# Small parts of split fp32r products multiplied as f16 copies, with a new instruction order, in a decoder layer

## The chip, the cores and the metric

One core of one Trainium2 chip runs the whole program. The metric is the device time of one execution in microseconds (us); each kernel was run several times and the median is given.

## What is computed

One pre-norm decoder layer in fp32 on x of 64 sequences × 128 tokens × 256. Cut to what matters:

```python
# self-attention: 64 sequences, one head, width 256
raw = (Q @ K.T) * scale                      # Q, K, V from layernorm(x)
w_attn = softmax(where(causal, -inf, raw)) @ V
c_attn = softmax(Q @ mean4(K).T * scale) @ mean4(V)
s_attn = softmax(scatter(top_k(raw, 64))) @ V  # 0 where not among the 64 largest
x = x + ((w_attn + c_attn + s_attn) / 3) @ Wo + bo
# cross-attention: 16 heads of 64, keys and values from ctx
x = x + (softmax(q @ k.T + mask) @ v) @ Wo
# feed-forward, both linear layers quantised per tensor to 8 bits
x = x + qlinear(gelu(qlinear(layernorm(x), w1, b1)), w2, b2)
```

The top-64 choice and the rounding in the quantised layers depend on small differences, so products are made to nearly full fp32 precision.

## The kernel before

**Tiling.** The 64 sequences go in 32 pairs. A pair's tiles are 128 partitions wide; an output bank of PSUM holds 128 × 512 fp32. `attentions` (L391) holds everything but the feed-forward stage, which `feed_forward` (L1600) does afterwards for all pairs.

**Pipeline.** Each engine has a function `body(i, front, back, ahead)` (L516 SP, L574 POOL, L728 PE, L1055 ACT, L1257 DVE), called for i = −1, 0, then in a loop of 30 (`Fori(1, PAIRS - 1)`), then 31 and 32. In one body three pairs are in work: *front* is pair i (cross-attention's keys, values, queries and scores, self-attention's output), *back* is pair i−1 (weighted values, heads, output product, x2 and its normalising), *ahead* is pair i+1 (layernorm of x, folded self-attention up to the mixed probabilities). The order in each body is written out by hand; engines meet only through semaphores. The bodies before the loop do part of the work in `EARLY_JOBS` while weights are still being prepared (`prepare_weights`, L116).

**Split products.** Each operand is kept as an fp32r upper part HI and an fp32r remainder LO. A product is three matmuls, HI·HI, HI·LO and LO·HI:

```python
def split_products(pe, out, lhs, rhs, last=True, first=True):
    pe.matmul(out, lhs[HI], rhs[HI], start=first, stop=False)      # L111
    pe.matmul(out, lhs[HI], rhs[LO], start=False, stop=False)      # L112
    return pe.matmul(out, lhs[LO], rhs[HI], start=False, stop=last)  # L113
```

The products that use it: `keys` and `queries` (four jobs each, 256 columns), `values` (four jobs, 512 columns), `output` (two, 256 columns), `fold_query` (the folded query g), `fold_value` (two), `raw_scores` (256 columns for each sequence: its own 128 keys and the other sequence's), and, on f16 operands, `weigh` (66 columns, "pv" in the order of the back) and `scores`. ACT writes HI from PSUM (`hi`, L1076; heads L1096), DVE writes LO from PSUM minus HI and frees the bank (`lo`, L1274; heads L1308). For keys and values ACT writes HI and an fp32 copy, and POOL makes LO (L581).

**DVE's other steps in a body.** `statistics` (L1231) and `normalise` (L1241) of a layernorm; `add_mask` (L1286, four heads a step, with their maxima); `row_sums` and `divide` (L1295, L1301, four heads); eight `top_round`s (L1335, L1338); `window_and_compressed` (L1347 to L1353); `mix` (L1367 to L1380) of the three softmaxes; `second_residual` (L1400, which makes x2) and `x2_statistics` (L1406, L1410). POOL subtracts the maxima (`shift`, L589), makes the LO part of the exponentials (`exp_lo`, L595) and the deviations of the layernorms (`x2_deviation`, L606 to L612, and L559 to L561).

**SP's queue.** In a body SP issues, each behind its own semaphore waits and in this order:

```python
if ahead: load_x(i + 1)                       # L497
if front: load_mask(1, i); load_mask(0, i)
if ahead: load_context(i + 1)
if back:  store_x2(0, i - 1); store_x2(1, i - 1)   # L510
if back:  store_normed(i - 1)                 # L514, waits for ACT's normalise_x2 (L1106)
```

So the load of the next x_in stands behind the store of the normalised x2. `statistics` of x_in waits for that load, and `load_x` for `normalise` of the x_in before.

## Time and profile before

| | |
|---|---|
| median of 3 runs | 1675.04 us (1672.29 to 1675.15) |
| profiled execution | 1671.48 us |
| its span, first to last instruction | 1669.4 us |
| mean granted TensorE clock | 0.983 of 2.4 GHz |
| PE busy | 1573.6 us, 94% |
| DVE busy | 1461.2 us, 88% |
| ACT / POOL busy | 1060.9 / 1051.2 us, 64% / 63% |
| DMA engines | 43 GB/s on average |

A line of the trace gives start, duration, engine, source line, operation, output<-inputs, shapes and type. Matmuls are pipelined, so their time is read from the distance between starts and not from the duration of one; where several stand in one line ("x15"), the time of the line is that of all of them. A bracket at a line's end is how long the engine stood idle before it, and what released it. The stretch from 131.9 to 1343.1 us is 28 turns of the loop. In trace lines the names of buffers have lost their numbers: `x2` reads x, `normed2` reads normed, `xn1` reads xn.

### The profile page before, as it was taken

Reading aid. Unit: us, or ns where it says so; the run is one execution under the profiler, and the core shown is the slowest. Engines: PE = TensorE matmul, PEld = TensorE weight load, DVE = VectorE, ACT = ScalarE, POOL = GpSimd, SP = SyncE. Lnnn points to the kernel's source line nnn. Section 1 sums busy time; section 2 is a strip of 40 time slices with the busy share of each in tenths; the row PEclk is TensorE's granted clock in tenths of the full one; section 3 lists DMA queues with packets and bytes.
Section 4 is the critical chain, followed back from the end, with each engine's and each line's share of the span. In section 5 each row is a group of like instructions: output and inputs, shape, how many; then the busy total and the mean of one; then the engine's idle time right before and its main releaser. Section 6 shows DMA issues by size and latency. Waiting matters only on the chain.

```text
span 1669.4 us, 51921 instructions
## 1 busy us (share of the span) xinstructions
PE 1573.6 (94%) x16058; PEld 1401.0 (84%) x16058; DVE 1461.2 (88%) x6184; ACT 1060.9 (64%) x2205; POOL 1051.2 (63%) x1168
## 2 busy tenths in 40 slices
PE   6799999999999999999999999999999999778898
PEld 5689999999999999999999999999999998644465
DVE  4889999999999999999999999999999996679876
ACT  4456666666666666666666666666666666469875
POOL 4557777777777777777777777777777776621000
PEclk9999999999999999999999999999999999789999
DMA  6000000000000000000000000000000000221155
GB/s 211 8 15 29 28 28 28 25 28 28 28 27 22 26 28 28 28 28 28 28 28 28 28 28 22 22 28 28 25 28 28 28 28 17 90 85 51 60 178 166
DMA packets 77732, 71.01 MB, mean 43 GB/s; under 512 B 6272, under 2 KB 77184, under 8 KB 77696
## 3 DMA queue, kind: packets, MB, share of 16 engines
q1 hardware_dynamic: 76736, 70.41, 13.4%
q8 instruction: 21, 0.34, 0.1%
q10 hardware_dynamic: 960, 0.13, 0.1%
q14 instruction: 15, 0.12, 0.0%
HBM read 45.36 MB, written 25.17 MB: 42 GB/s over the span
## 4 chain that ended last, share of the span: by engine, by line
PE 73%; DVE 14%; ACT 6%; issue 4%; POOL 1%; DMA 0%; ACTq 0%; DVEq 0%; SPq 0%; POOLq 0%
PE banks L111 21%; PE banks L112 18%; PE banks L113 18%; PE banks L868 5%; DVE tile_max L2010 4%; PE banks L848 3%; PE banks L892 3%; DVE xn L1241 3%; PE banks L1901 2%; ACT normed L1106 2%; DVE x L1390 1%; DVE ctx_t L1274 1%; ACT ctx_t L1076 1%; DVE kept L2022 1%; PE banks L747 1%
## 5 line engine op out<-in xcount | busy, mean ns | idle before, releaser
L589 POOL TENSOR_TENSOR shifted<-scores,score_max 128x512 f32<-128x512 f32 x256 | 266.9, 1043 | 200.6 <-DVE score_max L1286 159.9
L595 POOL TENSOR_TENSOR exp_t<-exp_copy,exp_t 128x512 f16<-128x512 f32 x256 | 302.5, 1182 | 60.6 <-ACT exp_copy L1091 60.6
L1286 DVE CUSTOM_DVE_ANT_0 scores<-banks,mask 128x128 f32<-128x128 f32 x1024 | 235.0, 286 | 11.6 <-issue 6.0
L1076 ACT ACTIVATE q_t<-banks 128x512 f16<-128x512 f32 x128 | 76.5, 598 | 224.0 <-PE banks L113 224.0
L581 POOL TENSOR_TENSOR v_nat<-kv_copy,v_nat 128x512 f16<-128x512 f32 x124 | 138.8, 1130 | 105.2 <-ACT kv_copy L1079 105.2
L111 PE MATMUL banks<-ctx_t,cross_Wk 128*128 128x256 f32 x512 | 154.7, 302 | 21.8 <-DVE ctx_t L1274 18.5
L1089 ACT ACTIVATE exp_t<-banks 128x512 f16<-128x512 f32 x256 | 155.9, 609 | 6.2 <-PE banks L113 3.8
L1091 ACT ACTIVATE exp_copy<-banks 128x512 f32<-128x512 f32 x256 | 158.6, 620 | 0.0
L868 PE MATMUL banks<-ident,shifted 128*128 128x128 f32 x1024 | 153.8, 279 | 3.9 <-POOL shifted L589 2.8
L111 PE MATMUL banks<-xn_t,cross_Wq 128*128 128x256 f32 x512 | 153.1, 299 | 2.7 <-POOL cross_Wo L269 1.6
L1079 ACT ACTIVATE kv_copy<-banks 128x512 f32<-128x512 f32 x248 | 150.9, 608 | 0.0
L1096 ACT ACTIVATE heads_t<-banks 128x512 fp32r<-128x512 f32 x128 | 76.5, 598 | 115.2 <-PE banks L892 115.2
L111 PE MATMUL banks<-cross_Wo,heads_t 128*128 128x256 f32 x512 | 147.8, 289 | 1.6 <-DVE heads_t L1308 1.6
L112 PE MATMUL banks<-ctx_t,cross_Wk 128*128 128x256 f32 x512 | 145.2, 284 | 0.0
L581 POOL TENSOR_TENSOR k_t<-kv_copy,k_t 128x512 f16<-128x512 f32 x124 | 145.1, 1170 | 0.0
L113 PE MATMUL banks<-xn_t,cross_Wq 128*128 128x256 f32 x512 | 145.1, 283 | 0.0
L113 PE MATMUL banks<-ctx_t,cross_Wk 128*128 128x256 f32 x512 | 145.0, 283 | 0.0
L112 PE MATMUL banks<-xn_t,cross_Wq 128*128 128x256 f32 x512 | 144.9, 283 | 0.0
L112 PE MATMUL banks<-cross_Wo,heads_t 128*128 128x256 f32 x512 | 144.3, 282 | 0.0
L113 PE MATMUL banks<-cross_Wo,heads_t 128*128 128x256 f32 x512 | 144.2, 282 | 0.0
L111 PE MATMUL banks<-v_nat,exp_t 128*128 128x66 f16 x1024 | 123.0, 196 | 6.5 <-POOL exp_t L595 3.3
L111 PEld LDWEIGHTS banks<-ctx_t,cross_Wk 128*128 128x128 f32 x512 | 97.8, 191 | 35.2 <-DVE ctx_t L1274 24.6
(261 smaller groups left out, 5661.8 us busy)
## 6 DMA issues: line engine op xcount, KB each, us to landing
x_in<-in_x_dram SPq DMA_DIRECT2D x32, 256.0 KB, 2.8
ctx_in<-in_ctx_dram SPq DMA_DIRECT2D x32, 256.0 KB, 2.7
x_residual<-x SPq DMA_DIRECT2D x64, 128.0 KB, 1.7
x_normalised<-normed SPq DMA_DIRECT2D x32, 256.0 KB, 2.1
shared<-x_normalised SPq DMA_DIRECT2D x8, 1024.0 KB, 5.3
shared<-x_residual SPq DMA_DIRECT2D x16, 512.0 KB, 3.8
out_dram<-shared SPq DMA_DIRECT2D x16, 512.0 KB, 2.9
mask<-in_fside_Bx1xSxS_dram SPq DMA_DIRECT2D x64, 64.0 KB, 1.8
```

The lines of the kernel that those rows point to most:

```text
L111: pe.matmul(out, lhs[HI], rhs[HI], start=first, stop=False)
L112: pe.matmul(out, lhs[HI], rhs[LO], start=False, stop=False)
L113: return pe.matmul(out, lhs[LO], rhs[HI], start=False, stop=last)
L581: pool.tensor_tensor(hilo(dst, *at)[LO], src, hilo(dst, *at)[HI], ALU.subtract).then_inc(kv_split, 1)
L589: pool.tensor_tensor(shifted[:, q % 2], scores[:, q % 2], score_max[:, q % 2, :].unsqueeze(2).to_broadcast([P, QUAD, P]), ALU.subtract).th ...
L595: pool.tensor_tensor(exp_t[:, q % 2, LO], exp_copy[:, q % 2], exp_t[:, q % 2, HI], ALU.subtract).then_inc(exp_split, 1)
L868: mm = pe.transpose(et_bank(q)[:, tile(h)], shifted[:, q % 2, h, :], ident)
L1076: op = act.activation(hilo(dst, *at)[HI], src, ACT.Copy)
L1079: act.activation(kv_copy[:, KV.index(k) % 2, :], fj_bank(k), ACT.Copy).then_inc(fj_free[k % 2], steps(k, same_bank(k), front, back, ahead, ...
L1089: act.activation(exp_t[:, q % 2, HI], et_bank(q).rearrange("p (h s) -> p h s", h=QUAD), ACT.Exp)
L1091: act.activation(exp_copy[:, q % 2], et_bank(q).rearrange("p (h s) -> p h s", h=QUAD), ACT.Exp).then_inc(et_free, 1)
L1286: op = dve.tensor_tensor_reduce(scores[:, q % 2, h, :], sc_bank(q)[:, tile(h)], mask[:, b, :], 1.0, NEG, ALU.add, ALU.max, score_max[:, q ...
```

## The change

1. **Small products in f16.** `half_products` first issues all HI·HI products of a job in fp32r, then for each term two products on f16 tiles: the f16 copy of HI on one side with the f16 LO of the other. LO tiles of keys', queries', values', outputs', folded and raw-score products are now f16. LO parts of weights are scaled up by 64 (256 for the folded ones), the copies of activations down by as much. `attend` and `weigh` keep the three-product form.
2. **Raw scores.** The small products cover only the sequence's own 128 keys.
3. **Copies.** ACT makes nine more SBUF-to-SBUF copies 128 × 512 in each body: of the transposed x (two), g, x1's transposed, the context, and four of the heads. In the preparation ACT makes 18 copies of weights and DVE scales 16 tiles of 512 columns.
4. **Order.** The job tuple, the back's order and the hand-written order on all five engines are new. The early jobs are only x, the four keys, g and the raw scores; the first pair's values are now made in body 0.

Cut to its core (`half` and `copy_heads` are new on ACT, `cross_halves` and `cross_up` in the preparation):

```diff
-(J_PT1, J_K0, J_K1, J_PT0, J_AO, J_X, J_K2, J_V0, J_V1, J_G, J_K3, J_X1, J_RAW, J_Q1,
- J_Q0, J_Q2, J_Q3, J_VV0, J_VV1, J_VV2, J_VV3, J_CTX) = range(22)
+(J_PT0, J_K0, J_K1, J_PT1, J_K2, J_AO, J_X, J_K3, J_V1, J_G, J_V0, J_RAW, J_X1, J_VV0,
+ J_Q1, J_Q0, J_Q3, J_VV1, J_Q2, J_VV2, J_VV3, J_CTX) = range(22)
...
-EARLY_JOBS = (J_X, J_G) + KV + (J_RAW,)
+EARLY_JOBS = (J_X, *J_K, J_G, J_RAW)
...
+def half_products(pe, terms):
+
+
+
+    for n, (out, left, right, *_) in enumerate(terms):
+        pe.matmul(out, left[0], right[0], start=(n == 0), stop=False, skip_group_check=True)
+    for n, (out, left, right, *narrow) in enumerate(terms):
+        small, cut = narrow[0] if narrow else (out, lambda t: t)
+        pe.matmul(small, left[1], cut(right[2]), start=False, stop=False, skip_group_check=True)
+        mm = pe.matmul(small, left[2], cut(right[1]), start=False, stop=(n == len(terms) - 1), skip_group_check=True)
+    return mm
...
+    def cross_halves(act, k0, k1):
+        act.wait_ge(cross_copied, k1)
+        for k in range(k0, k1):
+            act.activation(cross_at(k)[1], cross_at(k)[0].bitcast(F32), ACT.Copy).then_inc(cross_half, 1)
...
+            pool.tensor_tensor(cross_copy[:, k % COPIES, :], cross_copy[:, k % COPIES, :], cross_at(k)[0].bitcast(F32),
+                               ALU.subtract).then_inc(cross_low, 1)
+
+    def cross_up(dve, k0, k1):
+        for k in range(k0, k1):
+            dve.wait_ge(cross_low, k + 1)
+            dve.tensor_scalar(cross_at(k)[2], cross_copy[:, k % COPIES, :], UP, None, ALU.mult).then_inc(cross_split, 1)
...
             if front:
+                load_mask(0, i)
                 load_mask(1, i)
-                load_mask(0, i)
             if ahead:
                 load_context(i + 1)
             if back:
+                store_x2(1, i - 1)
                 store_x2(0, i - 1)
-                store_x2(1, i - 1)
                 store_normed(i - 1)
...
+        def raw_products(bank):
+
+            own = lambda b: (bank[:, b * 2 * P + b * P:b * 2 * P + (b + 1) * P], lambda t: t[:, tok(b)])
+            return half_products(pe, [(bank[:, b * 2 * P:(b + 1) * 2 * P], three(g_t, kt, tok(b)),
+                                       three(xn_t, kt, copy=PLAIN), own(b)) for b in range(2) for kt in range(DT)])
...
                 bank = begin(k)
-                for m, mt in enumerate(out_tiles):
-                    for kt in range(DT):
-                        mm = split_products(pe, bank[:, m * 2 * P:(m + 1) * 2 * P], hilo(w, kt, tile(mt)),
-                                            hilo(src, kt), first=(kt == 0), last=(kt == DT - 1))
-                done(mm, k)
+                done(half_products(pe, [(bank[:, m * 2 * P:(m + 1) * 2 * P], three(w, kt, tile(mt)), three(src, kt))
...
+        def half(k, part=HALF):
+
+            (top, halves), ready, scale = {J_X: (xn_t, plain_x if part == PLAIN else half_x, 1.0 / FOLD_UP),
+                                           J_G: (g_t, half_g, 1.0), J_CTX: (ctx_t, half_ctx, 1.0 / UP),
+                                           J_X1: (xn1_t, half_x1, 1.0 / UP)}[k]
+            act.activation(halves[:, part], top[:].bitcast(F32), ACT.Copy,
+                           scale=1.0 if part == PLAIN else scale).then_inc(ready, 1)
...
+            def copy_heads(c, n):
+                at = slice(4 * (c % 2), 4 * (c % 2) + 4)
+                act.wait_ge(bj_hi, bj_his(n, c))
+                act.activation(heads_t[1][:, HALF, at, :], heads_t[0][:, at, :].bitcast(F32), ACT.Copy,
+                               scale=1.0 / UP).then_inc(half_heads, 1)
...
+            if front:
+                exponential(1, i)
                 hi(J_VV3, i)
+            if ahead:
+                hi(J_CTX, i + 1)
+                copy(J_CTX, i + 1)
             if back and not front:
                 ffn_of["prime"](act)
             if back:
                 normalise_x2(i - 1)
-            if ahead:
-                hi(J_CTX, i + 1)
...
                     add_mask(2, i)
+                    add_mask(3, i)
                 if back:
                     second_residual(1, i - 1)
                     x2_statistics(i - 1)
-                if front:
-                    add_mask(3, i)
                 if ahead:
                     mix(i + 1)
+                if ahead and not front:
+                    early_lo(J_G)
                 if ahead and front:
                     lo(J_CTX, i + 1)
+                if front:
+                    add_mask(4, i)
                 if back:
                     largest_of_x2(i - 1)
-                if front:
-                    add_mask(4, i)
```

The order of instructions at three places in the loop, on DVE. `ISA` rows with `scores` and `score_max` are one head of `add_mask`.

DVE, the end of the loop body, before: the last head of `add_mask(3)`, then `mix`, the LO part of the context, and the largest of x2. The second residual and the x2 statistics stand ahead of this `add_mask(3)`.

```order
L1286 ISA score_max 128x1
L1367 RECIPROCAL inv_sums<-sums 128x6
L1369 TENSOR_TENSOR weights<-inv_sums,third 128x6
L1372 TENSOR_SCALAR win_in<-win_in,weights 128x128 x2
L1375 REGISTER_ALU
L1376 SCALAR_TENSOR_TENSOR sparse_in<-sparse_in,weights,win_in 128x128 x2
L1380 SCALAR_TENSOR_TENSOR probs<-comp_e,weights,sparse_in 128x128 x2
L1259 REGISTER_ALU
L1274 TENSOR_TENSOR ctx_t<-banks,ctx_t 128x512
L1415 ISA
L1415 TENSOR_REDUCE x2_far<-normed2 128x2
```

DVE, the same place after the change: `second_residual(1)` and `x2_statistics` now follow `add_mask(3)`; `mix` follows them.

```order
L1379 ISA score_max 128x1
L1488 REGISTER_ALU
L1493 TENSOR_TENSOR x2<-banks,x1_old 128x256
L107 REGISTER_ALU
L1499 BN_STATS stats2<-x2 128x6 x2
L1503 BN_AGGR moments2<-stats2 128x2 x2
L1460 RECIPROCAL inv_sums<-sums 128x6
L1462 TENSOR_TENSOR weights<-inv_sums,third 128x6
L1465 TENSOR_SCALAR win_in<-win_in,weights 128x128 x2
L1468 REGISTER_ALU
L1469 SCALAR_TENSOR_TENSOR sparse_in<-sparse_in,weights,win_in 128x128 x2
L1473 SCALAR_TENSOR_TENSOR probs<-comp_e,weights,sparse_in 128x128 x2
```

One step of four masks has moved ahead of the x2 statistics; the mix has stayed behind them.

DVE, the head of the loop body, before: the last head of `add_mask(5)`, then the statistics of x_in, then `row_sums(0)` (`inv_den`).

```order
L1286 ISA score_max 128x1
L1227 ISA
L1231 BN_STATS stats<-x_in 128x6 x2
L1235 BN_AGGR moments<-stats 128x2 x2
L1294 ISA
L1295 RECIPROCAL inv_den<-banks 128x4
```

DVE, the same place after the change: `row_sums(0)` and `divide(0)` (`heads_out`) come first.

```order
L1379 ISA score_max 128x1
L1387 ISA
L1388 RECIPROCAL inv_den<-banks 128x4
L1392 REGISTER_ALU
L1394 TENSOR_TENSOR heads_out<-banks,inv_den 128x4x64
L1320 ISA
L1324 BN_STATS stats<-x_in 128x6 x2
L1328 BN_AGGR moments<-stats 128x2 x2
```

The statistics of x_in, which wait for its load, have moved behind one row sum and one division.

DVE, `window_and_compressed`, before: behind the top round 6 and the LO part of queries 3 (`q_t`).

```order
L1338 MATCH_REPLACE left<-top8,left 128x128
L104 REGISTER_ALU
L1338 MATCH_REPLACE left<-top8,left 128x128
L1259 REGISTER_ALU
L1274 TENSOR_TENSOR q_t<-banks,q_t 128x512
L1347 ISA win_in,maxes<-raw,causal 128x128
L1347 ISA maxes 128x1
L1347 ISA win_in,maxes<-raw,causal 128x128
L1347 ISA maxes 128x1
L1350 TENSOR_REDUCE comp_in<-raw 128x64
L1353 TENSOR_REDUCE maxes<-comp_in 128x2
```

DVE, the same step after the change: behind the LO part of x1 (`xn1_t_half`) and top round 1.

```order
L1367 TENSOR_TENSOR xn1_t_half<-banks,xn1_t 128x512
L1428 MAX top8<-left 128x8 x2
L107 REGISTER_ALU
L1431 MATCH_REPLACE left<-top8,left 128x128
L107 REGISTER_ALU
L1431 MATCH_REPLACE left<-top8,left 128x128
L1440 ISA win_in,maxes<-raw,causal 128x128
L1440 ISA maxes 128x1
L1440 ISA win_in,maxes<-raw,causal 128x128
L1440 ISA maxes 128x1
L1443 TENSOR_REDUCE comp_in<-raw 128x64
L1446 TENSOR_REDUCE maxes<-comp_in 128x2
```

The window and the compressed scores now come five top rounds earlier.

## Rows read from the trace of the kernel before

**Rows 1.** The page: busy time of the engines; the chain that ended last.

```profile
PE 1573.6 (94%) x16058; PEld 1401.0 (84%) x16058; DVE 1461.2 (88%) x6184; ACT 1060.9 (64%) x2205; POOL 1051.2 (63%) x1168
...
PE 73%; DVE 14%; ACT 6%; issue 4%; POOL 1%; DMA 0%; ACTq 0%; DVEq 0%; SPq 0%; POOLq 0%
```

**Rows 2.** Windows: span, PE, PEld, DVE, ACT, POOL busy, PEclk, DMA share, GB/s; 28 pairs, one pair.

```profile
131.90:1343.10 1211.20, 1191.37 (x12998) 1104.02 (x12993) 1117.76 (x5210) 771.64 (x1765) 882.04 (x981) 1.00 0.09 27
703.31:746.53 43.22, 42.51 (x468) 39.45 (x467) 39.87 (x187) 27.56 (x63) 31.51 (x36) 1.00 0.09 27
```

**Rows 3.** Timeline of PE: start, us, engine, line, operation (an output job, pv, queries).

```profile
719.93 0.28 PE L113 MATMUL banks<-cross_Wo,heads_t 128*128 128x256 f32 x1
...
721.01 0.28 PE L113 MATMUL banks<-cross_Wo,heads_t 128*128 128x256 f32 x1
...
721.47 0.19 PE L113 MATMUL banks<-v_nat,exp_t 128*128 128x66 f16 x1
721.50 0.36 PE L111 MATMUL banks<-xn_t,cross_Wq 128*128 128x256 f32 x1
721.70 0.28 PE L112 MATMUL banks<-xn_t,cross_Wq 128*128 128x256 f32 x1
```

**Rows 4.** Timeline of PE: values, 512 columns.

```profile
729.66 0.39 PE L112 MATMUL banks<-cross_Wv,ctx_t 128*128 128x512 f32 x1
...
730.58 0.40 PE L113 MATMUL banks<-cross_Wv,ctx_t 128*128 128x512 f32 x1
```

**Rows 5.** Timeline of PE: bf16 products of the feed-forward stage.

```profile
1581.50 1.03 PE L1875 MATMUL banks<-xq_t,w_q 128*128 128x512 bf16 x4
1582.36 1.80 PE L1901 MATMUL banks<-w_q,shared 128*128 128x256 bf16 x15
```

**Rows 6.** Waits of DVE, then PE, 100 to 1390: total us, times, longest us.

```profile
DVE x L1400 <- PE banks L113: 11.6, 30, 0.4
DVE stats L1231 <- DMA x_in<-in_x_dram: 7.9, 28, 0.4
DVE row_rq L1272 <- ACT v_fold L1076: 6.5, 29, 0.2
DVE scores L1286 <- issue: 6.0, 31, 0.2
DVE inv_den L1295 <- PE banks L113: 5.8, 23, 0.4
...
PE banks L111 <- DVE ctx_t L1274: 18.5, 30, 0.6
```

**Rows 7.** Timeline of DVE, ACT and SP at the end of a pair.

```profile
735.28 0.25 DVE L1410 BATCH_NORM_AGGREGATE moments<-stats 128x2 f32<-128x6 f32 x2
...
736.40 0.19 DVE L1367 RECIPROCAL inv_sums<-sums 128x6 f32<-128x6 f32 x1
...
737.61 1.09 ACT L1106 ACTIVATE normed<-x,shift,rstd 128x256 f32<-128x256 f32 x2
...
738.84 0.38 SPq L514 DMA_DIRECT2D x_normalised<-normed  x1
739.88 0.41 SPq L497 DMA_DIRECT2D x_in<-in_x_dram  x1
...
742.62 0.75 DVE L1231 BATCH_NORM_STATS2 stats<-x_in 128x6 f32<-128x256 f32 x2 [0.23 <-DMA x_in<-in_x_dram]
```

**Rows 8.** Timeline of DVE: one of the `divide` steps.

```profile
700.53 0.42 DVE L1301 TENSOR_TENSOR heads_out<-banks,inv_den 128x256 f32<-128x256 f32 x1
```

**Rows 9.** Groups of ACT, 1430 to 1669: busy us, mean ns of one; idle before.

```profile
L1954 ACT ACTIVATE shared<-kept 128x1024 bf16<-128x1024 f32 x22 | 22.1, 1050 | 1.5 <-DVE kept L2022 1.5
```

**Rows 10.** Single lines of DVE: ns min/median/max, first and last start.

```profile
L1241 DVE TENSOR_SCALAR xn<-x_in,moments,rstd x64: 405/698/1366, 13.5 to 1351.9; 128x256 f32<-128x256 f32 x64
...
L1347 DVE CUSTOM_DVE_ANT_0 win_in<-raw,causal x64: 279/284/506, 45.7 to 1377.3; 128x128 f32<-128x128 f32 x64
...
L1380 DVE SCALAR_TENSOR_TENSOR probs<-comp_e,weights,sparse_in x64: 342/347/1218, 54.7 to 1387.0; 128x128 f32<-128x128 f32 x64
```

More of the change, by code:

```diff
@@ L984, in body @@
             if front:
-                queries(3, i)
-            if front and not early:
-                values(0, i)
-            if front:
-                exp_transpose(0, i)
+                values(1, i)
             if back:
@@ L992, in body @@
             if front:
+                queries(2, i)
+                exp_transpose(0, i)
+                values(2, i)
                 scores(1, i)
-            if front and not early:
-                values(1, i)
             if back:
@@ L1040, in early_job @@
                 op.then_inc(early_hi, 1)
+                act.wait_ge(early_hi, 1)
+                half(k)
                 return
@@ L1489, in body @@
                     ffn_of["weight_peak"](dve, 1)
+                if back:
+                    add_mask(7, i - 1)
+                    row_sums(3, i - 1)
+                    divide(3, i - 1)
                 if ahead:
```

469 lines of the change are left out of this document (259 added, 210 removed).

## Prediction

> **What bounds the kernel now.** I read the page first [rows 1]. TensorE (PE) is busy for 94% of the span and VectorE (DVE) for 88%; the chain that ended last lies on PE for 73% and on DVE for 14%. That looks like a PE kernel with DVE close behind, so a cheaper PE is worth what DVE lets through. The windows give the pace: 1211.20 us hold 28 pairs, 43.26 each, and the single pair from 703.31 takes 43.22, with PE busy 42.51, DVE 39.87, ACT 27.56 and POOL 31.51, and the clock at 1.00, which is 2.4 GHz [rows 2]. ACT has 15.7 us free in each pair. Busy shares do not say what DVE would allow, so I looked at the waits [rows 6]: in 30 pairs DVE waits for PE (x, inv_den), for ACT (row_rq), and once a pair for the DMA of x_in; the longest of those is 0.4 us, so every party is nearly just in time.
>
> The last of these waits matters, because it belongs to a **ring** [rows 7]. The x2 statistics end at 735.28 + 0.25 = 735.53. POOL then makes the deviation, ACT normalises (737.61 to 738.70), SP stores the result at 738.84, and only behind that store, in SP's order, stands the load of the next x_in, at 739.88. It lands when DVE's BATCH_NORM_STATS2 starts, at 742.62. So the stretch from x2 statistics to landed x_in is 7.09 us. The rest of the pair, 43.22 − 7.09 = 36.13 us, is what DVE does in its own order from those statistics of x_in to the next x2 statistics. The pace cannot be shorter than these two together, whatever PE does.
>
> **PE's part.** Steps between starts: fp32r, 256 columns, (721.01 − 719.93)/9 = 0.120 us [rows 3]; fp32r, 512 columns, (730.58 − 729.66)/4 = 0.230 [rows 4]. The trace has no f16 product of that width; the nearest are bf16, and I take theirs: (1.80 − 0.28)/14 = 0.109 for 256 columns and (1.03 − 0.40)/3 = 0.21 for 512 [rows 5], the single durations 0.28 and 0.40 being those of [rows 3, 4]. Per pair 112 small products of 256 columns (keys 32, queries 32, outputs 32, fold_query 8, fold_value 8) save 0.011 each, 1.23 us. The 16 of the values save 0.02 each, 0.32. The 8 of the raw scores shrink to 128 columns; a 66-column product steps 0.03 (721.47 to 721.50) [rows 3], so on the line from 66 to 256 columns 128 cost 0.056, and 8 × (0.120 − 0.056) = 0.51. Against it: the first fp32r product behind 66-column f16 ones takes 0.20 to its next (721.50 to 721.70), 0.08 more than usual [rows 3]. The new order puts five jobs there (keys 0, the second fold_value, fold_query, raw scores, queries 1) where two stood: 3 × 0.08 = 0.24. Sum: −1.8 us, a PE pace of **41.4**. The bounds: if the 0.08 belongs to any change from f16 to fp32r, up to 16 more of the 18 jobs pay it, 1.3 instead of 0.24, and the gain is 0.75; no row gives more than 2.1 (without the 0.24). I take the low price since the nearest row is a 66-column one, whose stationary loads have nothing to hide behind.
>
> The trace's 0.21 us at 512 columns is the number used. The Trainium skill (TensorE: Matmul & The Clock Gate, Back-to-back issue gap) states about 81 ns for 128 columns and 131 ns for 512 in a stream of load and product pairs. By it the values would save 16 × (230 − 131) ns = 1.6 us and the raw scores 8 × (120 − 81) ns = 0.3, 1.1 us a pair more in all on PE; rows 5 disagree, and the measurement decides.
>
> **DVE's part.** The order rows show what changes inside the 36.13 us section. Out of it goes row_sums and divide 0, now ahead of the x_in statistics: 0.42 [rows 8] and a reciprocal, 0.6. Into it comes add_mask(3), now ahead of second_residual(1): the same step of four heads runs from 735.53 to 736.40, 0.87 [rows 7]. The waits in it for PE, ACT and issue, 11.6 + 6.5 + 6.0 + 5.8 = 29.9 us in 30 pairs, 1.0 a pair [rows 6], mostly vanish when PE runs ahead: at most 1.0, at least 0.2 (the longest single kind staying); I take 0.9. Section: 36.13 − 0.6 + 0.87 − 0.9 = 35.5. Ring: ACT now does context HI and its copy before the normalising; a 1024-wide SBUF-to-SBUF copy takes 1.05 [rows 9], so a 512-wide one about 0.6 (an estimate, a 512-wide half and some fixed part), but it stands where ACT is idle anyway while POOL makes the deviation, so I book 0.1. Ring: 7.2. Together 42.7; with the masks' order on SP, mask 0 before 1 and store 1 before 0, at nothing (DMA share 0.09 [rows 2]), I take a pace of **42.6**, 0.6 under the present one. That is below the cover PE gives away (41.4), so DVE, waiting for x_in, ends the pair.
>
> The nine ACT copies cost 9 × 0.6 = 5.4 us of the 15.7 free: nothing, unless one stands ahead of something late. If that cover were gone, a copy's 0.6 would go on the pair. PE's 0.6 us wait for the LO part of ctx_t [rows 6] becomes longer, not shorter, since PE arrives earlier; it is no longer on the path.
>
> **Outside the loop.** ACT gets 18 weight copies, DVE 16 scalings of 512; values jobs leave the early stretch and their loads of POOL with them. Bounds: all 16 scalings on the path beside POOL, 16 × 0.9, +14; all the left-out early jobs saved, −6. I take +3. The feed-forward stage is untouched.
>
> **Sum.** 30 × (−0.6) + 3 = −15. The profiled execution took 1671.5 (span 1669.4); the median of three runs is 1675.0, 0.2% above, and I put the change on the median: **1660**. Within this case the low end has every wait gone, no 0.1 for the copy and −6 outside, 30 × (−0.7) − 6 = −27; the high end keeps all but 0.2 of the waits, a pace of 43.3 that rounds to no gain, and +3: **1648 to 1678**.
>
> **Rivals.** *A, the forecast above: 0.46.*
>
> *B, PE's pace is reached (0.22).* The section is full of DVE operations that POOL slows: normalising x_in takes 0.405 us at least, 0.70 at the median and 1.37 at most [rows 10]. If the new order lets two such pairs run clear, DVE gets back the 1.2 us between 42.6 and 41.4. Then 30 × (−1.8) + 3 = −51: **1624**. For it: window_and_compressed, lo and masks are all shuffled against POOL. Against it: POOL is busy 31.5 of 43 us, so most places collide.
>
> *C, slower (0.20): DVE meets POOL.* window_and_compressed moves from behind queries 3, late in the pair, to right behind the second top-k round, where POOL has exponentials' LO, keys 3 and values 0. One window operation takes 0.284 at the median and 0.506 at most [rows 10], a factor 1.8, which over the 1.0 us of the step is +0.8. Probs goes from 0.347 to 1.218 [rows 10], four such operations in the mix; the x_in pair from 0.8 to the 1.66 it already sometimes takes would be +0.7 more. Section and ring become 42.7 + 1.5 = 44.2: 30 × 1.0 + 3 = +33, **1708**. It decides against the change from 0.6 us of added blocking a pair upward. The trace shows such blocking at 1.218 against 0.347 us.
>
> The Trainium skill (SBUF — State Buffer, SBUF: two separate sides) has the rule behind it: a DVE operation with two SBUF inputs or in a 2-port mode and a GpSimd operation exclude each other for a whole instruction. The trace agrees with it for probs (two SBUF inputs). For the window operation it shows 0.506.
>
> *D, no gain appears (0.12).* The normalising moves by a whole copy's 0.6 rather than 0.1: 35.5 + 7.7 = 43.2, and the time is 1675 + 3 = **1678**. Or the changes between fp32r and f16 cost 0.08 in both directions: 18 jobs × 2 × 0.08 = 2.9 against 2.1 saved, a PE pace of 44.0 and 30 × 0.8 + 3 = +27, 1702. For it: every small product now sits between fp32r groups, and no row shows such a change inside a job. Against it: the change from f16 to fp32r behind a 66-column product is the only one that reads longer in [rows 3].
>
> **Chances.** About 0.2% (3.3 us) is what a measurement can tell from no change. Faster: A nearly whole (0.40) and B (0.22), 0.62. Same: the thin end of A and half of D, 0.09. Slower: C, half of D, and the end of A in which start-up and one late copy eat the gain, 0.29. The range runs from B's 1624 to 1702, leaving out the faster half of B and the far part of C. A's own is 1648 to 1678.
>
> **What would show it.** In the changed profile the pair should last about 42.6 us at clock 1.00, PE busy about 40.7, and the wait of DVE for x_in should grow from 0.26 us a pair to 1 or more, while DVE's waits for PE (x, inv_den) shrink: then A. If that wait is absent and PE is busy all but 0.7 us of the pair, B. If DVE's busy time per pair rises above 40.5 with window or probs operations near 0.5 or 1.2 us, C. Steps of the f16 products should read 0.109 and 0.21; a step of 0.12 or more there, or 0.20 at the first of every fp32r group, makes the PE term wrong and speaks for D. The forecast is wrong if the pair is over 43.2, or under 42.

## The result and the profile after

| | before | changed |
|---|---|---|
| median | 1674.3 us (1672.3 to 1675.2, 6 runs) | 1667.3 us (1665.6 to 1668.0, 6 runs) |
| ratio, 95% interval | | 0.9958 (0.9945 to 0.9971) |
| profiled execution: time, span | 1671.5, 1669.4 us | 1667.8, 1666.0 us |
| pace in the loop, from the context transposes of pair to pair | 43.25 us | 42.68 us |

The change makes the kernel 7.0 us faster, 0.42%, where 15 were forecast. The page after, busy time of the engines and the chain that ended last (compare [rows 1]):

```profile
PE 1554.7 (93%) x16058; PEld 1245.2 (75%) x16058; DVE 1468.4 (88%) x6202; ACT 1223.2 (73%) x2511; POOL 1062.8 (64%) x1168
...
PE 39%; DVE 34%; issue 12%; ACT 7%; DMA 4%; POOL 2%; DVEq 1%; SPq 1%; ACTq 0%; POOLq 0%
```

PE has lost 19 us of busy time in all, ACT has gained 162 (most of it the nine copies a pair), and the chain no longer lies on PE for 73% but on PE for 39 and DVE for 34. The windows after, of 28 pairs and of one (compare [rows 2]; span, then PE, PEld, DVE, ACT and POOL busy, clock):

```profile
141.80:1336.90 1195.10, 1169.46 (x12993) 964.56 (x12992) 1117.69 (x5209) 905.06 (x2017) 893.01 (x981) 1.00 0.09 28
696.60:739.30 42.70, 41.77 (x465) 34.44 (x464) 39.92 (x187) 32.34 (x73) 31.92 (x36) 1.00 0.08 28
```

The 28 pairs last 42.68 us each against 43.26, the single one 42.70 against 43.22. In the single one PE's busy time fell only from 42.51 to 41.77, and DVE's did not change (39.87 and 39.92). The waits of DVE from 100 to 1390 us (compare [rows 6]; total, times, longest), with the longest one before, which [rows 6] leave out, ahead of those after:

```profile
DVE ctx_t L1274 <- ACT ctx_t L1076: 26.0, 30, 0.9
```

```profile
DVE stats L1324 <- DMA x_in<-in_x_dram: 41.0, 29, 1.5
DVE raw L1412 <- PE banks L128: 6.4, 30, 0.2
DVE inv_den L1388 <- PE banks L116: 4.5, 2, 2.9
```

and those of PE:

```profile
PE banks L124 <- DVE g_t_half L1355: 10.1, 30, 0.3
PE banks L950 <- DVE heads_out L1394: 3.4, 15, 0.3
```

DVE's wait for x_in grew from 7.9 us in 28 pairs to 41.0 in 29; its waits for x and row_rq have all but gone (x 0.6 us in all, once). This is the picture that the forecast had described, but most of the growth has another source. Before, DVE also stood 0.87 us a pair for ACT's HI part of the context, between the x2 statistics and the statistics of x_in. ACT now makes that part ahead of the normalising, and this wait has gone (0.5 us, once). So DVE's idle time in that stretch rose from 0.87 + 0.26 = 1.13 to 1.41 us a pair, by 0.3 and not by 1.15. The ring, on the timelines of DVE, ACT, SP and DVE again (compare [rows 7]):

```profile
739.88 0.25 DVE L1503 BATCH_NORM_AGGREGATE moments<-stats 128x2 f32<-128x6 f32 x2
...
742.28 1.10 ACT L1183 ACTIVATE normed<-x,shift,rstd 128x256 f32<-128x256 f32 x2
...
743.51 0.38 SPq L571 DMA_DIRECT2D x_normalised<-normed  x1
744.55 0.41 SPq L554 DMA_DIRECT2D x_in<-in_x_dram  x1
...
747.28 0.75 DVE L1324 BATCH_NORM_STATS2 stats<-x_in 128x6 f32<-128x256 f32 x2 [1.35 <-DMA x_in<-in_x_dram]
```

From the end of the x2 statistics, 739.88 + 0.25 = 740.13, to the landed x_in at 747.28 are 7.15 us, and the rest of the pair, DVE's section, is 42.68 − 7.15 = 35.53. Forecast were 7.2 and 35.5.

What the small products cost PE, and what the entry into a job costs (timeline of PE; compare [rows 3, 5]):

```profile
716.03 0.19 PE L116 MATMUL banks<-v_nat,exp_t 128*128 128x66 f16 x1
716.56 0.71 PE L124 MATMUL banks<-xn_t,g_t 128*128 128x256 f32 x4 [0.34 <-DVE g_t_half L1355]
717.11 0.23 PE L127 MATMUL banks<-xn_t_half,g_t_half 128*128 128x128 f16 x1
...
717.24 0.22 PE L127 MATMUL banks<-xn_t_half,g_t_half 128*128 128x128 f16 x1
...
717.52 0.22 PE L128 MATMUL banks<-xn_t_half,g_t_half 128*128 128x128 f16 x1
...
723.01 0.27 PE L128 MATMUL banks<-xn_t_half,cross_Wq_half 128*128 128x256 f16 x1
723.04 1.19 PE L124 MATMUL banks<-cross_Wo,heads_t 128*128 128x256 f32 x8
724.07 0.28 PE L127 MATMUL banks<-cross_Wo_half,heads_t_half 128*128 128x256 f16 x1
```

In the raw scores the steps are (717.52 − 717.24)/5 = 0.056 us. From the last f16 product of 256 columns at 723.01 over eight fp32r ones to 724.07 are 1.06 us, which is 0.109 + 8 × 0.119: the change from f16 to fp32r costs nothing there. Behind the 66-column product at 716.03 it is otherwise: 0.03 for that product and 0.34 of waiting would put the first raw product at 716.40, it starts at 716.56, and its four take 0.55 instead of 0.48. This entry costs 0.23.

The single lines of DVE (ns min/median/max; compare [rows 10]):

```profile
L1334 DVE TENSOR_SCALAR xn<-x_in,moments,rstd x64: 401/405/411, 13.8 to 1348.6; 128x256 f32<-128x256 f32 x64
L1334 DVE TENSOR_SCALAR xn<-x,moments,rstd x64: 650/1246/1362, 67.5 to 1397.0; 128x256 f32<-128x256 f32 x64
...
L1440 DVE CUSTOM_DVE_ANT_0 win_in<-raw,causal x64: 280/284/1112, 46.0 to 1361.5; 128x128 f32<-128x128 f32 x64
...
L1473 DVE SCALAR_TENSOR_TENSOR probs<-comp_e,weights,sparse_in x64: 337/346/347, 57.8 to 1381.9; 128x128 f32<-128x128 f32 x64
```

Normalising x_in now runs clear of POOL everywhere, 0.405 at the median against 0.698; inside the loop the two operations of a pair went from 1.78 us to 0.81. Normalising x1 does not, 1.246. The window operation stays at 0.284 in nearly all its places although it moved, and probs at 0.346. Another operation took the place of x_in's, the one that forms the sparse scores, before and after:

```profile
L1357 DVE SCALAR_TENSOR_TENSOR sparse_in<-left,raw x32: 425/426/1123, 47.8 to 1380.3; 128x256 f32<-128x256 f32 x32
...
L1450 DVE SCALAR_TENSOR_TENSOR sparse_in<-left,raw x32: 424/1344/1346, 52.6 to 1374.8; 128x256 f32<-128x256 f32 x32
```

It costs 0.92 us more in each pair. In the pair shown above it starts at 734.55, 0.11 us behind an operation of POOL (`exp_lo`). The 0.97 gained at one place and the 0.92 lost at the other are why DVE's busy time did not change.

The start of the program, marked by the transposes of the context of the first, second and third pair (the third stands at the end of the loop's first turn), before:

```profile
34.97 1.05 PE L747 MATMUL banks<-ident,ctx_in 128*128 128x128 f32 x4
...
81.01 1.00 PE L747 MATMUL banks<-ident,ctx_in 128*128 128x128 f32 x4
...
131.95 0.65 PE L747 MATMUL banks<-ident,ctx_in 128*128 128x128 f32 x4
```

and after:

```profile
38.34 0.63 PE L798 MATMUL banks<-ident,ctx_in 128*128 128x128 f32 x4 [0.87 <-DVE raw L1412]
...
90.69 0.60 PE L798 MATMUL banks<-ident,ctx_in 128*128 128x128 f32 x4
...
141.85 0.60 PE L798 MATMUL banks<-ident,ctx_in 128*128 128x128 f32 x4
```

From the first of these marks to the third, called "to the loop" below, the program takes 103.5 us instead of 97.0. Nearly all of the 6.5 lies between the first two, 52.35 us against 46.04: PE is busy there for 37.35 us against 34.76 and idle for 3.7 us more, and the granted clock is 0.80 on average against 0.94. From the second to the third it is 51.16 against 50.94. The waits of PE in the first 142 us, after:

```profile
PE banks L926 <- ACT exp_copy L1168: 5.8, 2, 5.5
PE banks L124 <- DVE g_t_half L1342: 4.9, 1, 4.9
PE banks L124 <- ACT cross_Wk_half L296: 3.3, 1, 3.3
```

and the window from 57 to 81 us before, then after, with the granted clock as its third number from the end:

```profile
57.00:81.00 24.00, 15.84 (x162) 14.22 (x162) 19.52 (x99) 8.96 (x18) 11.96 (x13) 0.93 0.04 12
```

```profile
57.00:81.00 24.00, 16.03 (x92) 13.03 (x93) 16.57 (x61) 17.74 (x37) 12.16 (x11) 0.72 0.00 1
```

PE stood for g's LO part (4.9 us), for weight copies on ACT (3.3) and for an exponential that ACT makes only behind the next pair's softmaxes (5.5). The last of these lies behind the second mark, where PE stood for 4.1 us before the change too (for probs of DVE). In the window from 57 to 81 us the granted clock averaged 0.72 of 2.4 GHz against 0.93: part of it was spent at 1.2 GHz. The clock went to that level at 43.70, inside the 3.3 us of waiting, and again at 57.35, inside the 4.9 us, for 20.5 us in all between the first two marks (5.2 before). The end of the program, from the last such transposes on, takes 286.4 us against 283.1; over all profiles but e7's it takes 283.4 to 287.2 with the changed kernel and its variants, and 283.1 to 285.5 with the one before, so how much of these 3.3 us belongs to the change stays open; the means are 1.3 apart.

### The profile page after: what moved, and what is told of

It reads as the page before. It is cut to its first block, busy times and chain, and to the rows that moved or that the text cites. A ratio compares the mean times of both kernels' runs of the same rounds, so it can differ in the third digit from the quotient of the medians.

```text
span 1666.0 us, 52582 instructions
## 1 busy us (share of the span) xinstructions
PE 1554.7 (93%) x16058; PEld 1245.2 (75%) x16058; DVE 1468.4 (88%) x6202; ACT 1223.2 (73%) x2511; POOL 1062.8 (64%) x1168
## 4 chain that ended last, share of the span: by engine, by line
PE 39%; DVE 34%; issue 12%; ACT 7%; DMA 4%; POOL 2%; DVEq 1%; SPq 1%; ACTq 0%; POOLq 0%
PE banks L124 10%; PE banks L127 8%; PE banks L128 7%; DVE scores L1379 6%; DMA x_in<-in_x_dram 3%; DVE tile_max L2110 3%; DVE sparse_in L1450 2%; DVE heads_t_half L1401 2%; DVE xn L1334 2%; PE banks L926 2%; PE banks L906 2%; DVE left L1431 2%; PE banks L798 2%; PE banks L2001 2%; DVE g_t_half L1355 2%
## 5 line engine op out<-in xcount | busy, mean ns | idle before, releaser
L638 POOL TENSOR_TENSOR v_nat<-kv_copy,v_nat 128x512 f16<-128x512 f32 x128 | 149.3, 1166 | 44.5 <-ACT kv_copy L1146 44.5
L1166 ACT ACTIVATE exp_t<-banks 128x512 f16<-128x512 f32 x256 | 152.4, 595 | 5.7 <-PE banks L116 2.9
L114 PE MATMUL banks<-v_nat,exp_t 128*128 128x66 f16 x1024 | 121.9, 195 | 7.6 <-POOL exp_t L652 3.2
L926 PEld LDWEIGHTS banks<-ident,shifted 128*128 128x128 f32 x1024 | 115.2, 142 | 16.9 <-issue 7.6
L127 PE MATMUL banks<-ctx_t_half,cross_Wk_half 128*128 128x256 f16 x512 | 122.6, 279 | 0.0
L128 PE MATMUL banks<-ctx_t_half,cross_Wk_half 128*128 128x256 f16 x512 | 121.1, 276 | 0.0
L115 PE MATMUL banks<-v_nat,exp_t 128*128 128x66 f16 x1024 | 121.1, 195 | 0.0
L1431 DVE MATCH_REPLACE8 left<-top,left 128x128 f32<-128x128 f32 x448 | 120.2, 276 | 0.0
L114 PEld LDWEIGHTS banks<-v_nat,exp_t 128*128 128x128 f16 x1024 | 94.5, 97 | 34.2 <-issue 17.2
L127 PE MATMUL banks<-xn_t_half,cross_Wq_half 128*128 128x256 f16 x512 | 120.1, 275 | 0.0
L116 PE MATMUL banks<-v_nat,exp_t 128*128 128x66 f16 x1024 | 119.8, 193 | 0.0
L128 PE MATMUL banks<-xn_t_half,cross_Wq_half 128*128 128x256 f16 x512 | 118.7, 273 | 0.0
L127 PE MATMUL banks<-cross_Wo_half,heads_t_half 128*128 128x256 f16 x512 | 118.6, 278 | 0.0
L1143 ACT ACTIVATE k_t<-banks 128x512 f16<-128x512 f32 x124 | 74.0, 597 | 59.7 <-PE banks L128 59.7
```

The source lines that it names most:

```text
L127: pe.matmul(small, left[1], cut(right[2]), start=False, stop=False, skip_group_check=True)
L128: mm = pe.matmul(small, left[2], cut(right[1]), start=False, stop=(n == len(terms) - 1), skip_group_check=True)
L638: pool.tensor_tensor(hilo(dst, *at)[LO], src, hilo(dst, *at)[HI], ALU.subtract).then_inc(kv_split, 1)
L926: mm = pe.transpose(et_bank(q)[:, tile(h)], shifted[:, q % 2, h, :], ident)
L1166: act.activation(exp_t[:, q % 2, HI], et_bank(q).rearrange("p (h s) -> p h s", h=QUAD), ACT.Exp)
L1431: dve.match_replace(left[:, b, :], top8[:, b, :], (raw if r == 0 else left)[:, b, :], NEG).then_inc(top_out, 1)
```

## The experiments

The pace is always the distance of the context transposes from pair to pair in the loop. The changed kernel has 42.68 us and about 1667, the kernel before 43.25 and, run beside each group of experiments, 1672 to 1674. The ratios are to that kernel before. The theories are named in the expectations as they were held then; R and P were the first two.

**The ring cut, first try, in the changed kernel and in the one before.**

```diff
 # SP, end of body
-                store_normed(i - 1)
 # ACT, end of normalise_x2
+                act.wait_ge(normed_ready, n + 2)
+                act.dma_start(normed_pairs[n], normed2[:]).then_inc(normed_free, 16)
```

> The changed kernel with one edit: ACT issues the store of the normalised x2 on its own queue right after making it, so SP's load of the next x_in no longer stands behind it. Theory R (the ring: x2 statistics to landed x_in, 7.15 us, and DVE's section, 35.5, set the pace of 42.68 us): the load starts about 3 us earlier, DVE's wait for x_in falls from 1.42 us a pair to under 0.2, and the pace falls to what PE or DVE allow, 41.4 to 42.1; time 1667 - 30 x (0.6 to 1.3) = 1628 to 1649. Theory P (PE's work sets 42.68 and the wait for x_in is slack): pace stays 42.5 or more and time within 4 us of 1667.

> The same edit in the kernel before. Both theories take that kernel to be at PE's pace (43.2 with PE busy 42.5), with 0.26 us of waiting for x_in a pair. Theory R: the pace moves by 0.3 at most, time 1665 to 1674. If the ring was the bound there already, the pace drops by 0.5 or more, under 1660. Against 1674.3.

Measured: 1679.7 us (ratio 1.0043, 1.0027 to 1.0060), pace 43.25; and in the kernel before 1689.9 (1.0102, 1.0085 to 1.0119), pace 43.75. The waits of DVE, then PE, in the first:

```profile
DVE probs_t L1369 <- ACT probs_t L1143: 20.2, 54, 0.5
...
PE banks L124 <- DVE probs_t L1369: 19.3, 27, 0.7
```

The wait for x_in is gone, but ACT now stands about 1 us at its own store ahead of the probs_t of the next body, DVE behind ACT, and PE behind DVE with 0.7 us a pair. The edit bought one wait with another, so it decides nothing about the ring. It does show that ACT's first operation of a body is on the path.

**The ring cut on SP alone, in both kernels.**

```diff
 # SP, body
-            if ahead:
+            if early:
                 load_x(i + 1)
...
+            if ahead and not last:
+                load_x(i + 2)
+            if back:
                 store_normed(i - 1)
```

Here `early` is body 0 and `last` the loop's last turn, now written out behind it, which has no further x_in to load.

> The changed kernel with one edit on SP alone: the load of the x_in for the pair after next is issued at the end of a body, ahead of the store of the normalised x2 and not behind it. ACT's queue is as in the changed kernel, so what spoiled the run with the store on ACT (1 us more before its first copy of probs_t) is not there. Theory R (a loop of 42.68 us that runs x2 statistics, normalising, store, load, 7.15 us, and then DVE with 12 to 15 us of PE work in its middle): the 1.4 us wait for x_in goes and the pace falls by that or to PE's busy time, 41.6 to 42.2; time 1637 to 1653. Theory P (PE's work and its small waits set the pace): pace 42.5 to 42.7, time 1663 to 1670. Theory K (any change of phase brings new collisions of DVE with POOL): DVE busy above 40.3 us a pair and pace over 42.9.

> The same edit in the kernel before. Theories R and P: that kernel is at PE's pace, its 0.26 us wait for x_in goes and the pace falls by 0.3 at most: 1664 to 1675. Theory K: a pace above 43.4.

Measured: 1665.6 us (0.9952, 0.9936 to 0.9969), pace 42.68 as before the edit; the kernel before 1672.7 (0.9993, 0.9983 to 1.0002), pace 43.22. The waits of DVE in the changed kernel with this edit, 28 pairs:

```profile
DVE x L1487 <- PE banks L116: 17.6, 28, 0.6
DVE inv_den L1392 <- PE banks L116: 12.0, 28, 0.4
DVE probs_t L1371 <- ACT probs_t L1147: 7.4, 28, 0.3
```

The 1.4 us for x_in have become 0.63 for PE's attend (x), 0.43 for PE's pv (inv_den) and 0.26 for ACT's probs_t. Theory R, that the ring alone sets the pace, falls. DVE's timeline shows why, first in the changed kernel, then with the load ahead:

```profile
701.44 0.28 DVE L1367 TENSOR_TENSOR probs_t<-banks,probs_t 128x128 fp32r<-128x128 f32 x1
...
704.70 0.75 DVE L1324 BATCH_NORM_STATS2 stats<-x_in 128x6 f32<-128x256 f32 x2 [1.45 <-DMA x_in<-in_x_dram]
...
707.40 0.69 DVE L1483 TENSOR_TENSOR x<-banks,x_bias 128x512 f32<-128x512 f32 x1
```

```profile
698.44 0.28 DVE L1371 TENSOR_TENSOR probs_t<-banks,probs_t 128x128 fp32r<-128x128 f32 x1
...
704.39 0.69 DVE L1487 TENSOR_TENSOR x<-banks,x_bias 128x512 f32<-128x512 f32 x1 [0.63 <-PE banks L116]
```

From the LO part of probs 0 to the first residual, `x<-banks,x_bias`, are 5.96 us in the one and 5.95 in the other. In the first DVE comes there late from x_in and finds attend just done (its last product ends at 707.36), in the second it comes early and waits for attend. Both paths have the same length within what the trace resolves.

**More and less work on PE.**

```diff
 # e3, raw_products
-                                       three(xn_t, kt, copy=PLAIN), own(b)) for b in range(2) for kt in range(DT)])
+                                       three(xn_t, kt, copy=PLAIN)) for b in range(2) for kt in range(DT)])
 # e11, half_products, for the queries alone
-        pe.matmul(small, left[1], cut(right[2]), start=False, stop=False, skip_group_check=True)
+        if not fewer:
+            pe.matmul(small, left[1], cut(right[2]), start=False, stop=False, skip_group_check=True)
```

> The changed kernel with the small products of the raw scores over all 256 columns again: 8 products a pair go from 0.056 to 0.109 us, 0.42 us more PE work a pair. Theory R: PE has 0.9 us free a pair, pace within 0.1 of 42.68, time 1665 to 1671. Theory P: pace 43.1, time 1680.

> The changed kernel, leaving out one of the two small products of every term of the queries: 16 products of 256 columns a pair, 1.74 us of PE. Theory P2: PE's work sets the pace and with 1.74 less the next bound shows. If the ring of x_in and DVE's section is next, its slack in the changed kernel is the 1.4 us of waiting, and the pace stops near 41.3 with DVE waiting for x_in near 1.3 still; time 1667 - 30 x 1.4 = 1625. If PE still sets it: pace 40.95, time 1615. Theory S: pace 42.6 or more, 1664 to 1668.

Measured: e3 1677.6 us (1.0028, 1.0017 to 1.0039), pace 43.10, that is the whole 0.42. e11 1648.9 (0.9856, 0.9840 to 0.9872), pace 42.21: of 1.74 us taken off PE 0.47 arrive. The waits of DVE in e3, and the window from 151 to 1350 us and DVE's wait in e11:

```profile
DVE stats L1324 <- DMA x_in<-in_x_dram: 37.2, 27, 1.5
DVE raw L1412 <- PE banks L128: 17.9, 28, 0.6
```

```profile
151.00:1350.00 1199.00, 1152.98 (x12724) 933.80 (x12724) 1123.66 (x5279) 919.50 (x2046) 905.03 (x994) 1.00 0.09 28
...
DVE stats L1325 <- DMA x_in<-in_x_dram: 38.3, 28, 1.5
```

In e3 DVE waits 0.6 us for the raw scores instead of 0.2. In e11 PE is busy 1153.0 of 1199 us and idle for the rest, 1.6 us a pair, with DVE's wait for x_in unchanged. Compared step by step, 0.42 of the 0.47 comes where DVE takes a row sum and two LO parts of the queries: it starts them sooner, although the profile lists no wait there, and its busy time falls from 39.92 to 39.53 a pair. So the pace is not PE's work as such. Work on PE counts where DVE waits for its result, and the raw scores are such a place, while most of the queries are not.

**DVE work put outside and inside the stretch in question.**

```diff
+                for c in range(2):
+                    dve.tensor_reduce(at["spare"][:, bass.ds(n * 2 + c, 1)], keep["bo_row"][:], AX, ALU.max)
 # e18: behind lo(J_PT0, i); e19: behind add_mask(3, i), ahead of second_residual(1)
```

> The changed kernel with 0.7 us more of DVE work a pair (two maxima over 256 columns that nothing reads), put behind the LO part of probs 0, where DVE has 1.4 us of waiting for x_in ahead. Theory L: nothing moves, pace 42.68 to 42.75, time 1666 to 1670. If DVE's total work sets the pace: +0.7, time 1689.

> The same 0.7 us of extra DVE work, put behind add_mask(3) and ahead of the second residual, inside the stretch of DVE that theory L has in its loop. Theory L: the whole 0.7 goes on the pace, 43.4, time 1667 + 31 x 0.7 = 1689. If PE's work sets the pace: pace within 0.1 of 42.68, time 1667 to 1670.

Measured: e18 1673.7 us (1.0005, 0.9992 to 1.0018), pace 43.00; e19 1684.1 (1.0075, 1.0048 to 1.0102), pace 43.32. DVE's busy time rose by 0.47 and 0.65 a pair. The waits of e19, DVE then PE, and of e18:

```profile
DVE stats L1325 <- DMA x_in<-in_x_dram: 37.8, 27, 1.5
...
PE banks L872 <- DVE probs L1474: 20.9, 27, 0.8
```

```profile
DVE stats L1325 <- DMA x_in<-in_x_dram: 23.4, 27, 1.0
...
PE banks L799 <- DVE xn L1335: 23.0, 28, 0.8
```

Inside the stretch the whole 0.65 comes out at the pace, PE waits 0.8 us for probs, and the wait for x_in stays at 1.4. Outside it DVE's wait for x_in takes up 0.5, but 0.32 still comes out. This run is not as clean as it was meant to be: one of the two operations that normalise x_in now runs beside POOL and takes 1.25 us instead of 0.41 (at the same time those of x1 run clear, 1.1 less), so PE waits 0.8 us a pair for it, and DVE in turn 0.3 for g (`g_t_half <- ACT g_t`). So e19 comes out as a loop through this stretch wants it; e18 does not tell what the idle time ahead of x_in is worth by itself.

**Steps moved.**

```diff
 # e7, DVE: add_mask(3) behind x2_statistics again
 # e15, DVE: end of body
-                if front:
-                    add_mask(4, i)
 # e15, DVE: head of body, behind lo(J_PT0, i); POOL: shift(4, i - 1) behind exp_lo(1, i - 1)
+                    add_mask(4, i - 1)
 # e10, PE: raw_scores(i + 1) behind exp_transpose(7, i - 1), no more ahead of it
```

> The changed kernel with add_mask(3) back behind second_residual(1) and the x2 statistics on DVE, as before the change. Theory R: DVE's section is 0.87 us shorter, pace 41.8 if nothing else binds, 42.1 if DVE must wait for PE's output product; time 1641 to 1651. Theory P: pace 42.5 or more, time within 4 us of 1667, or slower since the shift behind this mask comes later.

> The changed kernel with add_mask(4) moved on DVE from the end of a body to the next body's head, behind the LO part of probs 0, and POOL's shift 4 moved along behind exp_lo 1. Theory L (a loop of 42.68 us: DVE without a wait from g's LO part and the raw scores to the LO part of probs 0, then PE from keys 0 to attend, then DVE's first residual, normalise and g; the wait for x_in lies beside PE's part and costs nothing): 0.87 us leave DVE's part and fall into DVE's 1.4 us of idle time beside PE's part, so the pace falls by up to 0.87, to 41.9 to 42.2 where PE's work binds; time 1641 to 1654. Theory R is dead; theory G (the pace is no loop but the sum of accidental collisions): any sign, pace 42.3 to 43.5.

> The changed kernel with one pair of neighbours exchanged on PE: raw_scores now stands behind the transposes of scores 7 and not behind pv5. By the starts in the changed kernel's trace an fp32r job behind 66-column products costs PE 0.08 to 0.25 us more than its products, and this one 0.24, while behind transposes of 128 columns it costs nothing; the pv5 to transpose change may take 0.03 to 0.16 back. Theory P2 (PE's work with these entries sets the pace): pace 42.68 falls by 0.1 to 0.24, time 1660 to 1664. Theory S (something that does not depend on PE's entries sets it): pace within 0.03 of 42.68; or raw scores come 0.44 us later and DVE waits: pace up by as much.

All three missed. e7: 1703.0 us (1.0185, 1.0167 to 1.0203), pace 43.83, DVE busy 40.79 a pair instead of 39.92. e15: 1757.1 (1.0512, 1.0484 to 1.0540), pace 44.55 in the first pairs and near 46 later. e10: 1682.6 (1.0059, 1.0042 to 1.0076), pace 43.27, DVE busy 40.49. In e15 this is PE's longest wait:

```profile
PE banks L798 <- DVE xn L1334: 54.1, 27, 2.0
```

POOL's and DVE's steps ahead of the normalising of x_in came later, and PE stood 2.0 us a pair at its transposes. In e10 the 0.23 of the raw entry went, entries of other jobs rose by more, and the raw scores came 0.1 later. What costs the time is one operation of DVE that now meets POOL: the second `win_in<-raw,causal` starts at 725.91, 0.02 us behind POOL's `v_nat`, and takes 1.25 us instead of 0.28, 0.96 a pair, against a pace that rose by 0.59. In e7 it is the first `win_in<-win_in,weights` of the mix, 0.95 instead of 0.29.

The larger part of e7's loss is the ring. POOL's order still has the shift of mask 3 ahead of the deviation of x2. With the mask behind the x2 statistics, POOL waits 1.55 us for its maxima and takes 1.05 for the shift, so the deviation begins 2.13 us behind the end of the statistics (753.84 against 751.71) and not 0.16 (740.29 against 740.13). Averaged over 20 pairs, the stretch from x2 statistics to x_in grows from 7.21 to 9.09 us, the rest of the pair shrinks from 35.47 to 34.73, and their sum is the measured 43.83: the edit did shorten DVE's section, and lengthened the ring by more. Moving one step of this order without the rest costs more than the step is worth.

**Interleaved as before.**

```diff
     for n, (out, left, right, *narrow) in enumerate(terms):
+        pe.matmul(out, left[0], right[0], start=(n == 0), stop=False, skip_group_check=True)
         small, cut = narrow[0] if narrow else (out, lambda t: t)
```

> The changed kernel with each term's two f16 products directly behind its fp32r product, as split_products has them, and not in a group of their own: 64 more changes from f16 to fp32r a pair. If such a change costs PE something everywhere (0.03 to 0.09 us), pace +2 to +5 us and time 1727 to 1820. If it costs only behind 66-column products, time within 4 us of 1667.

Measured: 1682.6 us (1.0058, 1.0041 to 1.0075), pace 43.28, between the two expectations. PE's busy time is 42.60 a pair, 0.83 more, over the 50 extra changes of a pair (68 terms in 18 jobs; the expectation's 64 was too many) 0.02 us each. That all fp32r products stand first is therefore needed: without it the changed kernel would be slower than the one before.

**The start-up.**

```diff
 # e5, DVE, body -1: cross_up(4, 8) from behind raw_scores to the end
 # e6, ACT: self_softmax(0) behind the early job of g; DVE: early_lo(J_G) ahead of mix
 # e13: both
```

> The changed kernel with the second four scalings of cross weights on DVE moved from behind raw_scores of body -1 to the end of that body. In the trace of the changed kernel DVE stands from 38.4 to 42.7 us at them, before the top rounds of pair 0. If these four are what made the start-up longer, 3 to 4.5 us of the 10 come back: 1663 to 1664.5; the loop's pace stays 42.68. If the start-up is set by what PE and ACT do, it stays within 1.5 us of 1667.

> The changed kernel with pair 1's early job for g moved ahead: ACT takes it before the softmaxes of pair 0 and DVE makes its LO part before the mix. PE waited 4.9 us for that LO part at 59 us. If that wait and the 5.5 us of PE at 91 us hang on the lateness of pair 1's raw scores, 4 to 8 us come back: 1659 to 1663; if the lost time lies elsewhere, within 1.5 us of 1667; pace 42.68 either way.

> Both start-up edits together: the second four scalings at the end of body -1, and the early job for g ahead of the softmaxes and of the mix of pair 0. From the first context transposes to the loop the changed kernel takes 103.5 us, 101.0 with the scalings late, 99.7 with g first, and the kernel before 96.9. If the two savings add, 97.2 and a time of 1660 to 1662; if they take the same time twice, 99.5 and 1663.

Measured: e5 1664.6 us (0.9947, 0.9930 to 0.9964), e6 1663.4 (0.9942, 0.9925 to 0.9958), e13 1665.0 (0.9949, 0.9932 to 0.9965); from the first mark to the loop 101.0, 99.7 and 103.4 us. The pace is 42.68 in all. The savings do not add, and e19, whose start-up has a little more DVE work than the changed kernel's, took 100.8 in its profile. The start-up scatters by some 2.5 us between executions, so e5 alone is not shown to gain. For g first the evidence is better: between the first two marks e6 takes 48.8 us, and e20 below, which has the same edit, 49.0, against 51.0 to 53.2 in every profile of the changed order without it. But e13, which has it too, took 52.2.

**The best of them beside the changed kernel.** e20 joins g first (e6) with the early load (e8); e21 is the changed kernel unedited on the same chip.

> The changed kernel with the early job for g ahead of the softmaxes and the mix of pair 0, and the load of x_in ahead of the store. From the earlier runs: g first takes 3.8 us off the start-up (99.7 against 103.5 us from the first context transposes to the loop), the early load nothing off the pace of 42.68. Expected 1663.5, 3 to 4 us under the changed kernel run beside it. If the start-up's length is only noise of the run, the two agree within 1 us.

> The changed kernel unedited, on the same chip beside e20, as its yardstick: 1667 within 2 us, start-up 103 to 104 us, pace 42.68.

Measured: e20 1661.4 us (0.9926, 0.9913 to 0.9940), e21 1666.1 (0.9949, 0.9935 to 0.9962); from first mark to loop 100.3 and 103.5 us. e20 is the fastest kernel here that makes all products (e11 leaves some out), 4.7 us under the changed one in medians, though the two intervals overlap a little. A last one, e15's edit with the early load and the late scalings, was a miss like e15:

> The same with the load of x_in ahead of the store and the second four scalings at the end of body -1. Theory L: if e15 gains, the wait for x_in would be late now (DVE's section holds add_mask 4, idle before x_in shrinks from 1.4 to 0.5), so the earlier load gives at most 0.3 more; start-up 2.5 us less: time 1637 to 1651, below e15 by 2 to 10. Theory G: no relation to e15 beyond the start-up.

Measured: 1760.7 us (1.0533, 1.0503 to 1.0563).

## Why the prediction was wrong

The direction, the range and the loop's pace were right, the pace partly by luck; the gain was 7.0 us where 15 were forecast. **The step that failed is the term "I take +3" for what lies outside the loop.** The loop's first turn gained nothing; 29 pairs at −0.57 give −16.6, forecast −18 for thirty. So the rest came to +9.6. In the trace 6.5 of it lie between the first mark and the third, 6.3 of them between the first two, and up to 3 behind the loop (286.4 us against 283.1, and against 284.3 in e9); what is left is within the scatter of the first mark, 33.6 to 38.4 us over all profiles. The +3 priced the added operations one by one. It did not follow who waits in that stretch, though the same reading was done for the loop: PE waits for the LO part of g, which DVE makes behind a mix, behind softmaxes, behind top rounds that start after four scalings; and the clock went to 1.2 GHz inside two of PE's waits. The bound of +14 did hold it. How much each of these waits is worth stays partly open, since e5, e6 and e13 do not add up.

By the other steps:

- **The products, right.** 0.109 and 0.056 us stand in the trace, and 0.216 for 512 columns in f16, where 0.21 was taken. Summed over a pair, the shorter steps save 1.85 us against 2.06 forecast.
- **The entries, too low.** 0.08 for three more jobs, 0.24, was taken. If every distance from a start to the next is added over a pair, less waits and steady steps, 1.1 us more remain after than before. That is close in size to the 1.3 that the forecast kept as its bound and did not take, though not by the bound's rule, since the entry behind 256 f16 columns cost nothing. The 0.23 of the raw scores shows the kind, an entry behind 66-column products at which PE also waits for another engine. PE's busy time so fell by 0.74 a pair and not by 1.8. This did not reach the time, as the pace was set elsewhere, but the forecast of PE at 41.4 was wrong.
- **DVE's section and the ring, right in size.** 35.53 and 7.15 against 35.5 and 7.2 (35.47 and 7.21 on average), the wait for x_in 1.4 us against "1 or more". The waits that vanished from the section came to 1.0, where 0.9 was taken. The rest of its size is luck: the forecast had neither the 0.97 that normalising x_in gave back nor the 0.92 that the sparse scores took. And the wait for x_in grew mainly because the one for ctx_t, in the same stretch, had gone, so its growth says little about PE running ahead. The high end of the section was added up too low: 36.13 − 0.6 + 0.87 − 0.2 + 7.2 is a pace of 43.4, not 43.3.
- **That this ring alone ends the pair, not so.** The ring does bind: e7 lengthened it, and the pace followed the sum of ring and section. But e8 took it away and the pace stayed at 42.68. A second loop is as long, as DVE's waits in e8 tell: DVE from g's LO part and the raw scores to the LO part of probs 0, PE from keys 0 to attend, DVE's first residual. e3 (+0.42 for 0.42) and e19 (+0.64 for 0.65) lengthen both loops and agree with it; e8 shows that it is not shorter than the ring, and e18, with its collision, does not measure the slack beside it. Whether a third path is as long was not tested.
- **The rivals.** B's time did not come: e11 shows that even a PE with 1.7 us less work stops at 42.21. C, the moved window beside POOL, did not come: 0.284 at the median. But both had part of their mechanism right. Normalising x_in did run clear, as B wanted, 0.97 us a pair, and a DVE operation did meet POOL anew, as C feared, though another than it named, 0.92 a pair; the two cancelled. D's 0.08 in both directions is refuted by the 1.06 us above, and by e12, where a change inside a job costs about 0.02.

## What to carry to other kernels

When the busiest engine gets less work, read off the order who hands work to whom around one turn of the loop, and count only the savings that lie on that circle: here 0.42 us of the raw scores counted in full and 1.74 us of the queries by a quarter. A wait that grows as forecast is not yet the bound; take it away alone and see whether the pace moves. Moving steps also changes which of DVE's operations meet POOL: compare every operation's duration before and after, since two such changes of 0.9 us can hide each other. And follow the start-up's waits with the same care as the loop's: here 6.5 us of the loop's 17 were lost there, and more than half outside the loop in all.

## What the runs showed beyond that

- fp32r products grouped ahead of f16 ones cost nothing at the change behind 256 f16 columns (1.06 us for one and eight), while alternating them cost 0.83 us of PE a pair.
- A store put on ACT's queue delayed the loop by 0.57 us a pair in the changed kernel and 0.5 in the one before, though ACT was idle for 10 and 16 us of each pair.
- Extra work of 0.65 us on DVE cost 0.64 us a pair at one place; at another it cost 0.32, with a new collision with POOL of 0.84 in it.
- One DVE operation, `sparse_in<-left,raw`, took 0.43 us in one order and 1.34 in another, where it started 0.11 us behind an operation of POOL.
